# Transposed attention scores as one float32 product of 512 columns per row group, and new orders of the steps on all engines, in a four-layer kernel on one core

## The reference, cut to what matters

```python
x = x + L0_ffn(L0_cond(x, cond_8, ...))
x = x + L1_ffn(L1_cond(x, cond_8, ...))
x = x + L2_ffn(L2_cond(x, cond_8, ...))
x = x + L3_ffn(L3_cond(x, cond_8, ...))

def L3_ffn(src, ...):                      # the part that the product of the change belongs to
    q = (src @ Wq).reshape(Bb, Tt, H, DH).transpose(0, 2, 1, 3)        # H 16, DH 8
    k = (src @ Wk_c @ Wk).reshape(Bb, Tt, H, DH).transpose(0, 2, 1, 3)
    v = (src @ Wv_c @ Wv).reshape(Bb, Tt, H, DH).transpose(0, 2, 1, 3)
    q = _apply_rope(q, sin, cos)
    k = _apply_rope(k, sin, cos)
    attn = jnp.einsum('bhqd,bhkd->bhqk', q, k) / np.sqrt(DH)
    attn = jax.nn.softmax(attn, axis=-1)
    sa = jnp.einsum('bhqk,bhkd->bhqd', attn, v)
    sa = sa.transpose(0, 2, 1, 3).reshape(Bb, Tt, C) @ Wo
    x = _rmsnorm(src + sa, norm1_w)
    ...                                    # shared expert, two of eight routed experts
    return _rmsnorm(x + shared + routed, norm2_w)
```

## Time and profile before

| what | value |
|---|---|
| median of 3 runs | 1083.67 us (1083.15 to 1088.16) |
| the profiled execution | 1086.03 us, of which the span is 1084.1 us |
| PE busy | 1007.2 us, 93% of the span, 6716 instructions |
| DVE busy | 724.3 us, 67% |
| ACT busy | 489.6 us, 45% |
| POOL busy | 175.2 us, 16% |
| chain that ended last | PE 61%, issue 25%, DVE 5%, ACT 3%, POOL 3% |

### The profile page before, as it was taken

One profiled execution on the slowest core, in us unless ns is written; L12 is line 12 of the kernel. 1 busy time (PEld: TensorE's weight loads), 2 busy tenths in 40 slices (PEclk: granted clock), 3 DMA queues, 4 the chain that ended last, 5 costly groups with the idle time before them and its releaser, 6 DMA issues.

```text
span 1084.1 us, 18147 instructions
## 1 busy us (share of the span) xinstructions
PE 1007.2 (93%) x6716; PEld 758.2 (70%) x6742; DVE 724.3 (67%) x1698; ACT 489.6 (45%) x818; POOL 175.2 (16%) x292
## 2 busy tenths in 40 slices
...
GB/s 351 1 31 16 16 1 16 16 16 15 2 136 1 54 15 49 60 59 2 136 136 1 1 1 3 116 1 1 2 1 7 6 1 6 1 6 1 6 6 10
DMA packets 11799, 35.38 MB, mean 33 GB/s; under 512 B 2570, under 2 KB 5818, under 8 KB 10944
## 3 DMA queue, kind: packets, MB, share of 16 engines
...
q10 hardware_dynamic: 1152, 1.05, 0.3%
...
HBM read 33.16 MB, written 1.06 MB: 32 GB/s over the span
## 4 chain that ended last, share of the span: by engine, by line
PE 61%; issue 25%; DVE 5%; ACT 3%; POOL 3%; POOLq 2%; DVEq 1%; another core or an unknown queue 0%; ACTq 0%
PE ps L1153 4%; PE ps L1064 4%; PE ps L1128 4%; PE ps L1039 4%; PE ps L853 4%; PE ps L1019 3%; PE ps L1304 3%; PE ps L1004 3%; PE ps L1215 3%; PE ps L1012 3%; PE ps L1195 3%; PE ps L863 2%; PE ps L1235 2%; PE ps L899 1%; PE ps L910 1%
## 5 line engine op out<-in xcount | busy, mean ns | idle before, releaser
L1978 DVE TENSOR_REDUCE arena<-ps 128x8 f32<-128x2048 f32 x32 | 73.3, 2290 | 20.4 <-PE ps L1195 20.1
L1512 ACT ACTIVATE arena<-ps 128x2048 f32<-128x2048 f32 x32 | 60.1, 1878 | 57.2 <-PE ps L1219 57.2
L1128 PE MATMUL ps<-uR,arena 128*128 128x256 f32 x256 | 73.8, 384 | 0.1
L1039 PE MATMUL ps<-arena,uR 128*128 128x512 f32 x128 | 66.7, 603 | 1.2 <-ACT arena L1457 0.8
L1064 PEld LDWEIGHTS ps<-arena 128*128 128x128 f32 x512 | 61.1, 191 | 5.3 <-issue 2.1
L1064 PE MATMUL ps<-arena 128*128 128x128 f32 x512 | 62.9, 276 | 0.1
L1153 PE MATMUL ps<-arena 128*128 128x256 f32 x256 | 61.7, 388 | 0.8 <-DVE arena L1932 0.5
L1304 PE MATMUL ps<-arena 128*128 128x512 f32 x128 | 61.0, 603 | 0.5 <-DVE yT L2047 0.5
L1485 ACT ACTIVATE arena<-ps 128x512 f32<-128x512 f32 x64 | 37.5, 599 | 51.2 <-PE ps L1129 50.8
L853 PE MATMUL ps<-arena 128*128 128x256 f32 x256 | 58.4, 386 | 0.6 <-DVE arena L1724 0.6
L1153 PEld LDWEIGHTS ps<-arena 128*128 128x128 f32 x256 | 47.4, 192 | 13.3 <-issue 5.4
...
## 6 DMA issues: line engine op xcount, KB each, us to landing
...
arena<-in_expert_w SPq DMA_DIRECT2D x2, 2048.0 KB, 10.7
...
```

Source lines behind the costliest of these rows:

```text
L1039: mm(high[:, c, :], uR[:, b, k * P:(k + 1) * P], phiC[:, col:col + 512], start=True, stop=False)
L1128: mm(o, phiC[:, st_ * P:(st_ + 1) * P], uR[:, b, :], start=True, stop=False)
L1512: av(pexp[:, t, gp].rearrange("p c h t -> p (c h t)"), scores[:, :, :].rearrange("p c t -> p (c t)"), ACT.Exp, scale=SCALE3).then_inc(s.sc ...
L1978: V.tensor_reduce(nm[:, k, :, 2 * gp:2 * gp + 2], scores[:, :, :].rearrange("p c (h t) -> p c h t", h=2), X, ALU.max, negate=True).then_in ...
```

## The change

Part one is in `step_d` of PE. Before, a TS step did for each half `h` of 256 columns four float32 products, one for each row group, and then four bf16 products that add minus the maximum. Now four float32 products of 512 columns cover both halves, and the eight bf16 products follow. The columns that pass are the same; 16 products become 12.

```diff
+                    for c in range(4):
+                        row = slice(32 * c, 32 * c + 32)
+                        mm(scores[:, c, :], kR[u][row, t * P:(t + 1) * P],
+                           qm[u][row, 2 * gp:2 * gp + 2, :].rearrange("p g t -> p (g t)"), start=True, stop=False)
                     for h in range(2):
-                        g = 2 * gp + h
                         for c in range(4):
                             row = slice(32 * c, 32 * c + 32)
-                            mm(scores[:, c, h * T:(h + 1) * T], kR[u][row, t * P:(t + 1) * P], qm[u][row, g, :],
-                               start=True, stop=False)
-                        for c in range(4):
-                            row = slice(32 * c, 32 * c + 32)
-                            last = mm(scores[:, c, h * T:(h + 1) * T], sel3[row, g, :], nmT[row, :], start=False, stop=True)
+                            last = mm(scores[:, c, h * T:(h + 1) * T], sel3[row, 2 * gp + h, :], nmT[row, :],
+                                      start=False, stop=h == 1)
                     last.then_inc(s.st_mm, 1)
```

```diff
-    MX1.0 Y1.1 MX2.0 CL5.2 Y2.1 MX3.0 Y3.1 CL6.2 NM.0 S.1 TS0.0 V.1 CL7.2 TS1.0 Q.1 K.1 TS2.0 AV0.0 TS3.0 CSUM.2
-    MX0.1 AV1.0 AVT0.0 Y0.2 AVT1.0 MX1.1 SAT.0 Y1.2 MX2.1 WO.0 Y2.2 MX3.1 X5T.0 FF0.0 G3.0 NM.1 TS0.1 Y3.2 FF1.0 S.2
+    CL5.2 MX2.0 Y2.1 MX3.0 Y3.1 CL6.2 NM.0 TS0.0 CL7.2 S.1 TS1.0 V.1 Q.1 TS2.0 CSUM.2 K.1 TS3.0 AV0.0 MX0.1 AV1.0
+    AVT0.0 MX1.1 AVT1.0 Y0.2 Y1.2 SAT.0 MX2.1 WO.0 Y2.2 MX3.1 X5T.0 Y3.2 FF0.0 NM.1 G3.0 TS0.1 FF1.0 S.2 Q.2 TS1.1
```

More of the change, by code:

```diff
@@ L115 @@
     "PE": """
[L116 to L125, removed]
@@ L126 @@
-    "ACT": """
[L127 to L131, removed]
@@ L138 @@
[L138 to L142, removed]
@@ L143 @@
[L143 to L146, removed]
+    COND.0 NT0.0 LOG0.0 WM.0 GTR0.0 COND.1 SPR0.0 NT0.1 QK.0 LOG0.1 SC.0 VT.0 PT.0 GTR0.1 AT.0 COND.2 SPR0.1 O1.0
+    QK.1 NT1.0 VT.1 SC.1 NT0.2 LOG1.0 LOG0.2 PT.1 MH0.0 MH1.0 AT.1 GTR1.0 SPR1.0 O1.1 MOE.0 GTR0.2 UG0.0 SPR0.2
@@ new lines @@
+    LOG1.5 MH0.5 MH1.5 DN.4 QK.6 GTR1.5 NT0.7 L1G.4 SPR1.5 LOG0.7 VT.6 SC.6 MOE.5 GTR0.7 PT.6 UG0.5 AT.6 SPR0.7 O1.6
+    UG1.5 QK.7 DN.5 NT1.6 SC.7 L1G.5 LOG1.6 MH0.6 PT.7 VT.7 MH1.6 GTR1.6 AT.7 SPR1.6 O1.7 MOE.6 UG0.6 NT1.7 LOG1.7
+    UG1.6 MH0.7 MH1.7 GTR1.7 DN.6 L1G.6 SPR1.7 MOE.7 UG0.7 UG1.7 DN.7 L1G.7""",
+    "ACT": """
+    AF0.0 GX0.0 GTR0.0 RW0.0 RW1.0 AF0.1 QKC.0 GX0.1 EX.0 VC.0 RX.0 PTC.0 GTR0.1 RW0.1 RW1.1 CV.0 AF1.0 QKC.1 VC.1
+    AF0.2 EX.1 GX1.0 PTC.1 GU0.0 GU1.0 GTR1.0 GX0.2 GTR0.2 SI0.0 RW0.2 AF1.1 RW1.2 GX1.1 SI1.0 QKC.2 DN.0 GTR1.1
@@ L150 @@
+    RG1.3 RG0.5 RA0.6 RA1.4 RG1.4 RG0.6 RA1.5 RG1.5 RA0.7 PX.0 RG0.7 RA1.6 RG1.6 RA1.7 RG1.7""",
 }
```

213 lines of the change are left out of this document (115 added, 98 removed).

## The result

The changed kernel takes 1067.48 us (median of 4 runs, 1066.85 to 1069.41), the kernel before 1083.53 beside it; the ratio is 0.9845, with a 95% interval of 0.9816 to 0.9875. In a second set of runs it was 1066.86 against 1086.47, 0.9826 (0.9800 to 0.9852). The forecast was faster, with 1076.8 as the time and 1068.0 as the lower end of the range. The direction was right, the gain was more than twice the net sum of 6.9 us, and the time lies half a us under the range.

What follows compares the result with a forecast made beforehand. PE, busy 93% of the span, bounds the kernel; six places where its waits close sum to 9.9 us, less 3 for new waits, net 6.9: 1076.8 us against the 1083.67 median, range 1068 to 1086.

Steps and rivals of the forecast that it cites:

- the term of nothing: Stage D, TS steps: fewer, wider float32 products take 1.19 to 1.29 us a step against 1.29; no change taken.
- a cost for each product: Rival, TS: each product costs something beside its columns, so 128 fewer save 3 to 6 us, 1073; chance 0.08.
- row groups in each other's way: Rival, TS: four row groups at 512 columns collide, 1105 at two together, 1084 at a quarter of that; chance 0.10.
- Start: Kernel start: LN0.0 ahead of WB.0 on DVE lets PE's transposes NT0.0 begin earlier; gain 1.15 us.
- First batches: Early stage A: LOG0.1 ahead of SC.0, MH.0 ahead of AT.1 and GTR1.0 fill PE's waits; gain 1.9 us.
- Entry of D: Entry of stage D: AV0.0 fills MX0.1's wait and Y3.2 moves into waits for DVE's maxima; gain 2.5 us.
- Last batches: End of stage D: RT2.5 behind TS0.7, so the DVE chain to FIN.5 and then FF0.6 come earlier; gain 1.6 us.
- End of A: End of stage A: LA.6 ahead of S8M0.7 on DVE lets MOE.7 start at 293.5, not 294.56; gain 1.06 us.
- the allowance: Whole kernel, stage A above all: 3 us set against the gains for new waits at places not followed.
- where I had counted 1.7: Middle of stage A: steps moved ahead of SC.5 and LOG1.6 fill their waits of 1.05 and 0.68 us; gain 1.7.
- the waits move and do not close: Rival, whole kernel: fillers only shift PE's waits, product alone left at nothing, 1081 to 1085 us; chance 0.32.
- the sign: Stage A: PE's idle time from 50 to 300 us still 14 us would show that waits only move.

Runs made afterwards that it cites:

- extra products: PE products nobody reads, put in waits from the end of stage A into stage B: changed kernel 1062.56 us, with five more 1063.01; kernel before, same products, 1080.97.
- first (product): Kernel before with the new TS product alone, old tables: 1083.36 us against 1084.63, ratio 0.9978.
- third (B and D): Kernel before with the new table of stages B and D alone: 1082.96 us, ratio 0.9975.
- second (A): Kernel before with the new table of stage A alone, on all engines: 1069.99 us against 1084.63, ratio 0.9841.
- fourth (both tables): Changed kernel with the old TS product, both new tables kept: 1069.39 us, ratio 0.9842 against the kernel before.
- the change again: The changed kernel, unaltered, measured again for comparison in the second set: 1066.86 us against 1086.47 for the kernel before.
- WB.0 back: Changed kernel with WB.0 ahead of LN0.0 again on VectorE: 1068.96 us, one run.
- PE's old order near the end: Changed kernel with PE's old order from RT1.5 to TS3.7, RT2.5 ahead of TS0.7 and RT3.5 ahead of TS1.7: 1071.42 us, one run.
- half of A: Kernel before with the new order of stage A in its first half alone, to NT0.5 on PE: 1081.99 us, ratio 0.9971.

## Why the prediction was wrong, point by point

**The product: right.** 1.29 us before and after, the term of nothing. The case of a cost for each product falls with it (128 fewer, and the step is as long); the case of row groups in each other's way falls too, at 0.96 us for the float32 part where 0.88 would be full overlap. The Trainium skill, "TensorE: Matmul & The Clock Gate", section "Measured speedup vs the span model", would have had 1.15 us there by my estimate; the trace does not agree with it.

**The places: right, the sizes in part.** Start 1.15, measured 1.10 as a wait and 0.74 in the pair of profiles. First batches 1.9, measured 2.17 over the whole window from 25.0 to 78.6. Entry of D 2.5: MX0.1's wait of 1.44 is 0.20 after, and DVE's maxima (L1978), 16.6 us earlier in batch 0 (706.04 to 689.46), are 19.1 us earlier in batch 2 (776.39 to 757.28), 2.5 us more. But 1.7 of it is a half-clock stretch of before (from 753.70, 3.42 us busy, half of it lost), which the sum did not have, so that the waits gave some 0.8. After, MX0.1 on PE:

```profile
717.90 1.15 PE L1196 MATMUL ps<-x1C,arena 32*128 32x256 f32 x16 [0.20 <-ACT arena L1513]
```

Last batches 1.6: FF0.6 came 20.5 us earlier than before, 1.4 more than those maxima in batch 2, and then the clock took it back. End of A 1.06: idle time there fell by 1.12, but not where I put it. I had MOE.7's wait shrink because LA.6 came first; it went over to S8M0.7 and shrank by 0.16. The gain came one step ahead: before, PE waited 1.47 us for GU1.7 ahead of SPR1.7, in the change it waits 0.64 for DN.6 ahead of L1G.6. Before:

```profile
291.27 1.15 PE L842 MATMUL ps<-arena,cst 32*128 32x256 f32 x16 [1.47 <-ACT arena L1370]
```

**The step that failed: the allowance.** I took 3 us off for new waits at places I had not followed. From 78.6 to 279.5 us, where I had counted 1.7, PE's idle time fell by 4.6 (3.90 to 1.60 and 3.79 to 1.50). The small waits of stage A did not move about, they closed with the large ones. The gross sum of 9.9 stands against 10.3 us less idle time over the whole span of the pair; the net of 6.9 was the wrong number to forecast from. That 9.9 and 10.3 agree is partly luck: stage A gave 8.6 us where I had counted 5.8, and all that follows gave 1.7 where I had counted 4.1. There new waits did come: from 757.0 to 1012.8 us PE was idle for 0.95 us before (255.80 less 254.85), in the same piece after, 738.5 to 993.95, for 2.22 (255.45 less 253.23).

Of the rivals, "the waits move and do not close" is refuted by the windows of stage A, 8.6 us. But the sign that the prediction gave for it, 14 us of idle time from 50 to 300 us, did come true, 250.00 less 236.13:

```profile
50.00:300.00 250.00, 236.13 (x1555) 205.41 (x1554) 142.84 (x584) 122.06 (x201) 26.33 (x44) 0.98 0.05 15
```

The sign was badly chosen: since stage A is over at 298.23, the window holds the whole piece from MOE.7's start on, with its 6.0 us of idle time, where before it held the first 5.4 us of that piece. MOE.7 came at 283.17, 6 us ahead of the 289 to 292 that I had given.

**The step that was missing: the clock.** Fewer waits also meant fewer stretches at half clock. The sum had no term for that; the range's lower end had what is left of 8.8 us (1076.8 to 1068.0) behind the 3 of the allowance and the 4 of a price per product, under 2 us. In the pair of profiles it is 9.4 us of lost work time less. That pair shows too much of it, since the clock differs from execution to execution. The profiled executions of the kernels without extra products, with stage A in one order or the other throughout (but for WB.0 in one), let one divide the gain; of each, PE's idle time, half of its busy time at half clock (lost), and the rest of its busy time (work), in us:

| kernel | stage A | idle | lost | work |
|---|---|---|---|---|
| before | old | 76.9 | 19.3 | 987.9 |
| first (product) | old | 76.7 | 15.0 | 988.5 |
| third (B and D) | old | 77.8 | 19.8 | 984.0 |
| second (A) | new | 68.3 | 14.8 | 987.7 |
| fourth (both tables) | new | 68.9 | 12.8 | 984.9 |
| the change | new | 66.6 | 9.9 | 988.5 |
| the change again | new | 66.5 | 9.9 | 988.6 |
| WB.0 back | new | 69.1 | 11.2 | 986.7 |
| PE's old order near the end | new | 67.8 | 13.0 | 988.8 |

The work is the same within 5 us whatever the order, so that half is about the right price of half clock. On the mean, idle time falls from 77.1 to 67.9 us with the new table of stage A, by 9.3, and lost time from 18.0 to 11.9, by 6.1, which makes 15.4 of the measured 16.0. So two terms failed: the waits gave 9.3 where I had a net 6.9, and the clock some 6 where I had nothing in the sum. The 6 are the less certain number, as the lost times of one table differ by up to 5 us.

Part of the clock is the order's. With the old table of stages B and D all five profiled executions have a stretch at half clock at the entry of stage D (from 753.70 before, 751.41 in the first kernel, 740.18 in the second, 750.14 with half of A, 748.54 with extra products in before), with the new one none of nine. Four of the five with the old order in the middle of stage A have one a few us behind the wait of SC.5 (197.33, 197.09, 193.76, 195.58), of the nine with the new order none. Other places, as those in the first and the fourth kernel show, are the execution's own.

The experiments with extra products show directly that the clock, from the end of stage A to the first steps of stage B alone, is worth 4 to 5.5 us in either order. And since the two orders differ by 18.0 us with extra products in both and by 19.6 without, the clock of that stretch is no large part of what the change gave, 1.6 us by these medians.
